# Gated linear attention with a feed-forward block: another order of the instructions at the end of row 0's attention

## What is computed

```python
q, k, v = x @ Wq, x @ Wk, x @ Wv                       # 16 heads of 8
gate = exp(log_sigmoid(x @ Wgk1 @ Wgk2 + bgk2) / 16)   # per token and key element
state = state * gate + v ⊗ k                           # scan over the 512 tokens
out_t = state · q_t
out = layernorm(out) * gamma + beta
out = out * silu(x @ Wg)
x = layernorm(x + out @ Wout)
h = silu(x @ w1 * s1) * (x @ w2 * s2)                  # 128 -> 512
h = gelu(h @ h1 * s3); h = gelu(h @ h2 * s4)           # 512 -> 512, twice
x = layernorm(x + h @ w3 * s5)                         # 512 -> 128
```

## Time and profile before

| what | us |
|---|---|
| time, median of 3 runs | 193.87 |
| lowest and highest of the 3 runs | 193.68 and 195.78 |
| the profiled execution's own time | 193.71 |
| its span from first to last instruction | 191.9 |
| busy TensorE, VectorE, ScalarE, GpSimd | 162.0, 147.9, 117.5, 113.8 |

### The profile page before, as it was taken

The page is one execution under the profiler, slowest core; times in us unless marked ns, Lnnn a source line. Parts: engine busy times, 40 slices in busy tenths (PEclk is TensorE's granted clock), DMA queues, the critical chain, the costliest instruction groups (busy, mean ns, idle before and its releaser), DMA issues.

```text
span 191.9 us, 2751 instructions
## 1 busy us (share of the span) xinstructions
PE 162.0 (84%) x790; PEld 124.0 (65%) x790; DVE 147.9 (77%) x301; ACT 117.5 (61%) x188; POOL 113.8 (59%) x94
## 2 busy tenths in 40 slices
PE   1859988969499997999999699999987999799840
PEld 1638656849387774878768487677856866567630
DVE  1398886988788997998999997899999685512360
ACT  4633649898037725378682556768454688979623
POOL 8989589919706689580677688427782313470011
PEclk9999999999979999999999999999999999999996
DMA  3999700000000000000000010000000100002002
GB/s 119 332 419 405 274 3 0 0 0 3 0 3 0 0 2 0 3 2 0 0 0 0 0 41 14 0 0 0 3 0 0 56 0 0 0 0 60 0 3 58
DMA packets 6191, 8.65 MB, mean 45 GB/s; under 512 B 513, under 2 KB 5026, under 8 KB 5666
## 3 DMA queue, kind: packets, MB, share of 16 engines
q1 hardware_dynamic: 5602, 5.60, 9.1%
q0 software_dynamic: 576, 2.88, 3.9%
HBM read 7.43 MB, written 1.05 MB: 44 GB/s over the span
## 4 chain that ended last, share of the span: by engine, by line
PE 25%; DVE 18%; issue 8%; ACT 5%; POOL 4%; DVEq 1%; POOLq 0%; ACTq 0%
PE ffn L600 8%; PE ffn L591 8%; DVE state L994 5%; DVE y L1005 2%; DVE y L1009 2%; DVE f_lo L1091 1%; ACT f_hi L831 1%; PE ffn L569 1%; DVE o_acc L1012 1%; DVE ffn L1080 1%; PE att L526 1%; POOL u_tok L313 1%; PE ffn L574 1%; ACT f_hi L839 1%; POOL o_rstd L332 1%
## 5 line engine op out<-in xcount | busy, mean ns | idle before, releaser
L354 POOL TENSOR_TENSOR f_lo<-full,f_hi 128x512 fp32r<-128x512 f32 x20 | 26.0, 1315 | 30.4 <-DVE full L1080 19.5
L994 DVE TENSOR_TENSOR_SCAN state<-gate,att 128x512 f32<-128x512 f32 x32 | 38.4, 1210 | 3.0 <-PE att L515 3.0
L839 ACT ACTIVATE f_hi<-ffn,vec_cols 128x512 fp32r<-128x512 f32 x32 | 22.1, 690 | 27.4 <-PE ffn L600 27.2
L591 PE MATMUL ffn<-f_hi,h_hi 128*128 128x512 f32 x128 | 36.7, 405 | 1.7 <-ACT f_hi L831 1.3
L600 PE MATMUL ffn<-f_lo,h_hi 128*128 128x512 f32 x128 | 35.6, 399 | 0.0
L591 PEld LDWEIGHTS ffn<-f_hi,h_hi 128*128 128x128 f32 x128 | 23.5, 188 | 8.7 <-ACT f_hi L831 3.0
L1091 DVE TENSOR_TENSOR f_lo<-ffn,f_hi 128x512 fp32r<-128x512 f32 x28 | 18.9, 687 | 12.4 <-ACT ffn L842 11.4
L600 PEld LDWEIGHTS ffn<-f_lo,h_hi 128*128 128x128 f32 x128 | 23.9, 188 | 5.8 <-DVE f_lo L1091 0.4
L313 POOL TENSOR_TENSOR u_tok<-kv_tok 128x1024 f32<-128x1024 f32 (+1 forms) x12 | 27.3, 2282 | 0.5 <-issue 0.4
L328 POOL TENSOR_TENSOR o_acc<-o_acc,y 128x512 f32<-128x512 f32 x16 | 20.6, 1290 | 7.9 <-DVE y L1005 7.8
L1005 DVE TENSOR_TENSOR y<-att,state 128x512 f32<-128x512 f32 x32 | 21.1, 671 | 0.0
(11 more groups left out here) (162 smaller groups left out, 318.6 us busy)
## 6 DMA issues: line engine op xcount, KB each, us to landing
h_raw<-in_hT SPq DMA_DIRECT2D x2, 1024.0 KB, 11.3
h_hi<-in_hT POOLq DMA_DIRECT2D x2, 1024.0 KB, 11.7
x_tok<-in_x SPq DMA_DIRECT2D x4, 256.0 KB, 5.0
out<-out_tok SPq DMA_DIRECT2D x3, 256.0 KB, 2.3
w_raw<-in_w12T SPq DMA_DIRECT2D x1, 512.0 KB, 4.6
w_hi<-in_w12T POOLq DMA_DIRECT2D x1, 512.0 KB, 8.1
xT_raw<-in_xT SPq DMA_DIRECT2D x1, 256.0 KB, 2.6
proj_raw<-in_proj SPq DMA_DIRECT2D x2, 128.0 KB, 2.3
```

The source lines that it names most:

```text
L354: nc.gpsimd.tensor_tensor(lo[:, o], full_block(layer, o), hi[:, o].bitcast(F32), ALU.subtract).then_inc(pool_rested, 1)
L591: nc.tensor.matmul(bank[:], h_hi[:, layer - 1, c, tile(o)], src_hi[:, c], start=(c == 0), stop=False)
L839: nc.scalar.activation(hidden[layer][0][:, o], bank[:], ACT.Gelu, scale=scales[:, 1 + layer, o:o + 1]).then_inc(gelu_hi_ready, 1)
L994: nc.vector.tensor_tensor_scan(state[:, k % 3], gate[:, b], A[2 + k % 2][:], 0.0, ALU.mult, ALU.add).then_inc(scanned, 1)
```

## The change

It changes the order of four queues between about 23 us and 55 us, and with it two banks. Nothing is computed otherwise.

- Bank and place of row 3's q: `project_q(3)` writes A[1] instead of F[0], waits for the last `read_out` (which frees A[1]), and stands ahead of `transpose_o(0)` instead of behind `project_beta(0)`. The banks of g for rows 1 to 3 are F[0], F[2], F[3] instead of F[2], F[3], F[0].
- TensorE: `project_g(1)` goes ahead of `project_beta(0)`; `project_out(0)` and `count_lo` directly behind it, ahead of `project_g(2)`. `count_lo` waits for the lo part of row 3's q, since it writes the same bank. The first block of `ffn_in` waits for two `add_beta_part`, the second for all four.
- ScalarE: four of the six `sum_lo` go further ahead: 0 and 1 in front of `gates(1)`, 2 and 3 around `gates(2)`, 4 behind `gates(3)`, 5 behind `fold_beta`.
- VectorE: `lo_any` directly behind `apply_gate(0)`, `flag_lo` and one `add_beta_part` ahead of `x2_normalise(0)`, one `add_beta_part` behind `rest_of_x2(0)`.
- GpSimd: the first outer product of row 1 waits for `o_ready`, the end of L1012.

The full diff:

```diff
--- before.py
+++ after.py
@@ -245,8 +245,8 @@
         X_BANK = (None, F[0], F[1], F[2])
         Z_BANK = (A[3], F[3], F[0], F[1])
         KV_BANKS = ((A[1], A[2]), (F[3], F[2]), (F[3], F[2]), (F[3], F[2]))
-        Q_BANK = (A[0], F[0], F[0], F[0])
-        G_BANK = (F[1], F[2], F[3], F[0])
+        Q_BANK = (A[0], F[0], F[0], A[1])
+        G_BANK = (F[1], F[0], F[2], F[3])
         U_ON_DVE, LATER_U_ON_DVE = (2, 3), 1
         block = ctx.enter_context(nc.Block())
 
@@ -368,6 +368,8 @@
                     sum_over_k(b + 1, (1, 2))
 
             def attention_end(a, tiles, follows):
+                if isinstance(a, int) and a == 0:
+                    pool.wait_ge(o_ready, 1)
                 if follows:
                     outer_products(a + 1, (0,))
                 o_rstd_of(a)
@@ -472,14 +474,12 @@
 
             def project_q(b):
                 pe.wait_ge(proj_lo_ready, 3)
-                if b == 1:
-                    pe.wait_ge(z_log_ready, 3)
-                elif b >= 2:
-                    pe.wait_ge(q_lo_ready, b)
+                if b >= 1:
+                    pe.wait_ge(*((z_log_ready, 3), (q_lo_ready, 2), (y_ready, DH))[b - 1])
                 project(b, 2, Q_BANK[b], q_ready)
 
             def project_g(b):
-                pe.wait_ge(*((z_log_ready, 4), (kv_copied, 2 * B), (kv_copied, 2 * B - 1), (q_lo_ready, B))[b])
+                pe.wait_ge(*((z_log_ready, 4), (q_lo_ready, 3), (kv_copied, 2 * B), (kv_copied, 2 * B - 1))[b])
                 project(b, 3, G_BANK[b], g_ready)
 
             def replicate_q(b, k):
@@ -557,7 +557,9 @@
                 if o == 0:
                     pe.wait_ge(x2_hi_ready, b + 1)
                     if isinstance(b, int) and b == 0:
-                        pe.wait_ge(beta_part_added, B)
+                        pe.wait_ge(beta_part_added, 2)
+                if o == 1 and isinstance(b, int) and b == 0:
+                    pe.wait_ge(beta_part_added, B)
                 if o == 1:
                     pe.wait_ge(yT_ready, b + 1)
                 if o >= 2:
@@ -643,7 +645,7 @@
 
             def count_lo():
                 pe.wait_ge(lo_any_ready, 1)
-                pe.wait_ge(y_ready, DH)
+                pe.wait_ge(q_lo_ready, B)
                 for n in range(WG):
                     last = nc.tensor.matmul(A[1][0:1, 0:1], lo_any[:, n:n + 1], ones[:], start=(n == 0),
                                             stop=(n == WG - 1))
@@ -744,18 +746,18 @@
             project_q(2)
             project_g(0)
             project_kv(3)
+            project_q(3)
             transpose_o(0)
             center_o(0)
+            project_g(1)
             project_beta(0)
-            project_q(3)
-            project_g(1)
+            project_out(0)
+            count_lo()
             project_g(2)
-            project_out(0)
+            project_beta(1)
             project_g(3)
-            project_beta(1)
             project_beta(2)
             project_beta(3)
-            count_lo()
             pe.wait_ge(lo_flag_ready, 1)
             exact = pe.value_load(lo_flag[0:1, 0:1], min_val=0, max_val=1)
             with pe.If(exact):
@@ -904,28 +906,28 @@
             round_x(2)
             log_part(1)
             round_x(3)
+            sum_lo(0)
+            sum_lo(1)
             gates(1)
             log_part(2)
             log_part(3)
+            sum_lo(2)
             gates(2)
-            sum_lo(0)
+            sum_lo(3)
             copy_kv(1)
             round_q(1)
             gates(3)
+            sum_lo(4)
             copy_kv(2)
             round_q(2)
-            sum_lo(1)
             copy_kv(3)
             nc.scalar.preload_act_table_set(SILU_SET)
             silu_of_g(0)
             fold_beta()
-            sum_lo(2)
-            sum_lo(3)
+            sum_lo(5)
+            silu_of_g(1)
             round_q(3)
-            sum_lo(4)
-            silu_of_g(1)
             silu_of_g(2)
-            sum_lo(5)
             silu_of_g(3)
             round_x2(0)
             for o in range(OB):
@@ -1209,17 +1211,17 @@
             o_token_stats(0)
             o_mean_and_variance(0)
             apply_gate(0)
+            dve.wait_ge(lo_summed, WG)
+            nc.vector.tensor_scalar(lo_any[:], lo_sums[:], 0.0, 1.0, ALU.not_equal, ALU.mult).then_inc(lo_any_ready, 1)
             rest_of_q(3)
             add_beta_part(0)
             add_x(0)
-            dve.wait_ge(lo_summed, WG)
-            nc.vector.tensor_scalar(lo_any[:], lo_sums[:], 0.0, 1.0, ALU.not_equal, ALU.mult).then_inc(lo_any_ready, 1)
-            x2_normalise(0)
             flag_lo()
             add_beta_part(1)
+            x2_normalise(0)
             add_beta_part(2)
+            rest_of_x2(0)
             add_beta_part(3)
-            rest_of_x2(0)
             scan(1, 0)
             scan(1, 1)
             read_out(1, 0)
```

## The result

| | before | changed |
|---|---|---|
| median, us (9 runs each) | 194.04 | 191.57 |
| lowest to highest | 193.41 to 195.78 | 190.92 to 192.99 |
| ratio, with its 95% interval | | 0.9867 (0.9833 to 0.9901) |
| span of the profiled execution | 191.9 | 189.8 |

1.3% less, 1.0% to 1.7% by the interval; 191.7 us had been forecast. The forecast took 2.0 us off 193.7; the profiled executions differ by 2.1 us and the medians by 2.5. What lies between the last two is not traced to a cause.

A forecast was written before the change was run, and what follows sets the result against it. A chain through row 0's attention end, longest in TensorE's 2.68 us wait for the flag, was taken to bound the kernel. 0.70 + 1.90 - 0.60 = 2.00 us off 193.71 gave 191.7; 8-in-10 range 190.8 to 192.7.

The forecast's parts named there:

- ScalarE's sums ahead of the copies: ScalarE, before `copy_kv(1)`: a second sum delays the copy by 0.60 us and row 0's last scan by 0.54.
- GpSimd behind `o_ready`: VectorE's last sums in row 0: without GpSimd's outer product beside it, L1009 takes 0.69 us, a gain of 1.13.
- q_lo and `add_x`: VectorE, lo part of row 3's q and the addition after it: q_lo at 43.74 instead of 44.29, `add_x` 0.96 us earlier.
- `r_var` under the outer product: VectorE before x2: GpSimd's outer products hold `r_var` until 48.0, shrinking the gain at x2 from 0.96 to 0.70 us.
- The flag ahead of x2: TensorE before x2's transposes: no wait for the flag, so x2's start to its rounding takes 1.72 instead of 3.62, gain 1.90.
- The last of beta's parts: VectorE, behind x2's lo part: one `add_beta_part` now on the way to row 1's first scan, cost 0.60 us.
- the clock's two: TensorE's clock falls anyway, 192.1 us, chance 0.15; or stays low through row 0's first feed-forward layer, 196, chance 0.05.
- the argument from the length of the idle time: TensorE before x2's transposes: a 1.81 us gap kept the clock, 2.68 didn't, so about 1 us should keep it.
- The rival that more comes back: The copy costs nothing (0.54 us), or TensorE pulls row 1's scans along (0.5): 190.6 to 191.2, chance 0.12.
- the branch itself holds TensorE: Before x2's transposes, fetching code behind the branch, not the flag, causes the wait; 1.9 us gain lost, 193.6, chance 0.03.

The follow-up runs named there:

- e6: Changed kernel with the ScalarE sums of groups 3 and 4 each one place later, so one sum less ahead of the copies of row 1's k and v: 192.19 us.
- e11: Changed kernel with ScalarE rounding row 3's q ahead of row 1's silu: 191.95 us.
- e3: Kernel before with only GpSimd's wait for `o_ready` added: 193.94 us, ratio 1.0006 to the kernel before.
- e2: Changed kernel without GpSimd's wait for `o_ready`: 192.65 us.
- e4: Kernel before with the flag made early and ScalarE's queue ordered as in the changed kernel, TensorE's projections left as they were: 194.55 us.
- e1: Changed kernel with `flag_lo` and one `add_beta_part` put behind `x2_normalise(0)` again: 193.34 us.
- e5: Changed kernel with the last `add_beta_part` ahead of x2's lo part again: 191.27 us.
- e7: Changed kernel, with GpSimd's second lo part of the hidden layer in row 1 also waiting for `o_ready`: 190.71 us.
- e9: Changed kernel with the last `add_beta_part` ahead of x2's lo part and GpSimd's `o_ready` wait also in row 1: 190.72 us.
- e10: Changed kernel with the last `add_beta_part` ahead of x2's lo part and GpSimd's `o_ready` wait also in rows 1, 2 and 3: 190.53 us.

## Why the prediction was right

The sum of the prediction was 0.70 + 1.90 - 0.60 = 2.00 us at the first scan; 2.08 were measured. Step by step:

- *ScalarE's sums ahead of the copies:* 0.54 at the last scan forecast, 0.50 measured. It was right at its place. As a cost on the way to the end it can't be taken alone: e6 gives 0.49 back at the last scan, puts the sum into ScalarE's later queue and loses 0.22 at the first scan, while e11 shows that the branch from `o_acc` over GpSimd is just as long. (The section on the change says that four of the six sums go ahead; its own list and the diff have all six.)
- *GpSimd behind `o_ready`:* L1009 at 0.69, a gain of 1.13 at that instruction, was right (e3). In the changed kernel the wait is worth 0.61 at the first scan (e2), since L1009 would begin later there and be held for less. I had given it no share of its own at x2, since q_lo waits for ScalarE, though the outer products that I placed at 43.66 hang on `o_acc`; by them it comes through. The wait and the rest of the change need each other: x2 starts 0.11 us earlier with the wait alone (e3), 0.24 with all but the wait (e2), and 0.85 with both. That two operands in SBUF are what counts has a control in the same place: the two read-outs ahead of L1009 have one operand in PSUM, and took 1.26 us with the outer product beside them (before, 36.52 to 37.78) and 1.26 without it (changed).
- *q_lo and `add_x`:* q_lo 0.55 forecast and 0.71 measured; `add_x` 0.96 and 0.90. The table load came only 0.48 later, not 0.60, and `add_x` follows q_lo by 1.43, not 1.21.
- *`r_var` under the outer product:* right in kind, too dear in size. I had it start at 47.58 and end at 48.0, 0.26 longer than its 0.16; it took 0.21, 0.05 longer. Counted from the mark it started 0.06 later than forecast, the outer product ended 0.07 earlier, and it ended 0.02 behind that instead of 0.10. The last two make the 0.15 by which x2 is earlier than forecast, 0.85 instead of 0.70. In e2 and e11 the same 4 columns take 0.56 and 0.62 and end within 0.03 us of the outer products. The rule of the Trainium skill ("SBUF — State Buffer", "Who interferes with whom") that the second of the two waits for the first one's end agrees with each of them. The sums of 512 columns end 0.54 or 0.55 us behind GpSimd's instruction (before, e2, e4, and `o_acc` of row 1 in the changed kernel). I take that for work of their own after the release, which no run tests.
- *The flag ahead of x2:* from x2's start to its rounding 1.72 forecast, 1.78 measured. The step in between was wrong: I had the reading of the flag follow beta's last product, at 49.3, and the branch end at 50.35. It began at 47.7, with products in TensorE's queue up to 48.86, and what ended TensorE's wait at 49.11 was x2, so branch and reading were over by then. TensorE's sequencer reads ahead of the products that it has handed on. The error did not matter, as x2 was later than both. The 1.84 gained here are the flag's 1.38 (e1) and 0.46 more, nearly all of it clock: from the start of the transposes to x2's lo part it is 1.77 us in the kernel before, and 1.34 in e3, where they ran at the high clock. These 0.43 are luck. e3 has the same idle time in front of the transposes and didn't pay them, so the change removes them only from such executions of the kernel before as have them, and the profiled one was one.
- *The last of beta's parts:* 0.60 forecast; with it x2's lo part and the first scan are 1.21 apart instead of 0.60. Moving it back gains 0.55 (e5). So the change has a loss of half a microsecond in it.

Together, by the marks: 0.85 up to x2, 1.84 from there to its lo part, 0.61 lost behind it, 0.85 + 1.84 - 0.61 = 2.08. The nearness to 2.00 is in part luck too: 0.15 too little at x2 stands against 0.06 too much from x2 to its rounding. Undone one at a time, the flag's place is worth 1.38, GpSimd's wait 0.61 and beta's part -0.55; with the 0.43 of clock that is 1.87, and 0.21 are left for the other moves (row 3's q, the banks, the rest of ScalarE's and TensorE's order), which no run takes out singly.

Of the rivals, neither of the clock's two came: the changed kernel's granted clock is 1.00 from 46 to 61 us. But the argument from the length of the idle time was not borne out (below). The rival that more comes back had two sources. The copy was not free, as the last scan came 0.50 later; and row 1's scans gained nothing of their own, 2.08 at the first and 2.09 at `o_acc`. That the branch itself holds TensorE is refuted by the 0.25 us of idle time that x2 ends, with the flag early, and by the 1.38 us that come back with the flag late (e1).

## What to carry to other kernels

A value that steers a branch is best made as soon as its inputs are there, with work queued behind it on the engine that branches: here that hides reading and branch wholly, and was worth 1.38 us. Pull it forward only with all queues that feed it, for the same flag made early in one set of queues and not in TensorE's order was 0.2 us slower than no change. And look at every VectorE instruction with two operands in SBUF on the critical chain, for what GpSimd runs beside it: one wait on GpSimd took 0.9 us out of a row (e7), though it can move the conflict on to the next such instruction, even one of 4 columns.

## What I had not expected of the hardware

- TensorE's clock fell after 1.50 us without work (e4, 0.8 us into the next work, at 52.8) and after 1.76 (e9), and stayed up after 2.26 (e1), in executions of nearly the same program. In the kernel before it fell within the idle time of 2.68, and in e3 that of 2.69 passed without a fall, which came 0.5 us behind it. The idle time before it does not decide it alone. The window of e4:

```profile
53.00:55.00 2.00, 1.85 (x9) 1.56 (x9) 2.00 (x4) 0.59 (x1) 0.56 (x1) 0.50 0.03 8
```

- Executions of nearly the same program drift apart before the change has any effect: row 0's first scan starts at 17.42 or 17.43 us in all thirteen, and its third read-out between 24.41 and 25.97. The eight transposes at 15.96 took from 1.33 us (e5) to 1.92. The granted clock doesn't tell these cases apart: between 16 and 17 us it shows 1.00 in e1 and 0.50 in e3, and the transposes take 1.91 us in both. Two such profiles are best compared behind a common mark.
- A VectorE instruction on 128x4 elements can take 1.12 us instead of 0.16 beside a GpSimd instruction (e10).
